# First attention of a two-layer decoder block: scores as three passes of rounded halves instead of one fp32 product

## The reference, cut to what matters

```python
q = rms_norm((x @ wq).reshape(B, L, 16, 128), q_norm_w)
k = rms_norm((x @ wk).reshape(B, L, 4, 128), k_norm_w)
k_ctx = rms_norm((h_ctx_kv @ wk_ctx).reshape(B, T, 4, 128), k_norm_w)
q = q * cos + rotate_half(q) * sin
k = k * cos + rotate_half(k) * sin
k_full = jnp.repeat(jnp.concatenate([k_ctx, k], axis=1), 4, axis=2)
scores = jnp.einsum('blhd,bmhd->bhlm', q, k_full) * scale + mask   # the product that is changed
probs = softmax(scores)
out = einsum('bhlm,bmhd->blhd', probs, v_full) @ wo
```

## Time and profile before

| | |
|---|---|
| three runs | 1883.96, 1883.88, 1882.28 us; median 1883.88 |
| the profiled execution | 1885.15 us, of it a span of 1883.4 us between the first and the last instruction |
| first attention | about the first 1000 us of the span |
| granted TensorE clock | 0.986 of full speed over the span |

### The profile page before, as it was taken

How to read it: one execution, slowest core, us unless ns; L and a number is a source line. 1 busy time by engine, 2 the same in 40 slices (tenths; PEclk the granted TensorE clock), 3 DMA queues, 4 the chain that set the end, 5 groups by cost and what they waited for, 6 DMA issues and landing times. The chain is left out here.

```text
span 1883.4 us, 27617 instructions
## 1 busy us (share of the span) xinstructions
PE 1771.8 (94%) x9732; PEld 1313.5 (70%) x9732; DVE 1093.9 (58%) x2271; ACT 1041.9 (55%) x2318; POOL 961.5 (51%) x864
## 2 busy tenths in 40 slices
PE   7899999999999999999998999989999778879998
PEld 4677777777777777777775888879899656644443
DVE  5554544456445664456655658633433668868886
ACT  3666666655555555555554322136656367857875
POOL 5644565444654445554441100038888356657774
PEclk9999999999999999999999999999999989999999
DMA  7111111211011111011121200157889660000000
GB/s 248 58 48 46 51 36 46 69 33 52 36 40 37 51 53 52 20 34 52 53 68 44 109 23 23 45 183 227 231 224 278 173 162 1 1 6 18 23 23 23
DMA packets 113607, 141.30 MB, mean 75 GB/s; under 512 B 38000, under 2 KB 68720, under 8 KB 113280
## 3 DMA queue, kind: packets, MB, share of 16 engines
q1 hardware_dynamic: 106304, 122.76, 20.7%
q0 software_dynamic: 7168, 16.78, 4.2%
HBM read 104.91 MB, written 29.36 MB: 71 GB/s over the span
## 5 line engine op out<-in xcount | busy, mean ns | idle before, releaser
L767 POOL TENSOR_TENSOR a_xcl<-xT,a_xch 128x512 fp32r<-128x512 f32 x64 | 82.9, 1295 | 282.5 <-ACT a_xch L565 282.5
L876 PE MATMUL a_S<-a_kT,a_qT 128*128 128x288 f32 (+3 forms) x640 | 207.8, 423 | 7.0 <-ACT a_qT L598 5.4
L683 DVE TENSOR_REDUCE a_nmax<-a_S 128x1 f32<-128x192 f32 (+3 forms) x256 | 138.2, 550 | 55.6 <-PE a_S L877 55.2
L934 PE MATMUL a_A<-a_pT,a_vf 128*128 128x512 f32 x320 | 167.0, 604 | 0.9 <-ACT a_pT L586 0.8
L571 ACT ACTIVATE a_pr_odd<-a_S,a_nmax 128x320 f32<-128x320 f32 (+1 forms) x128 | 80.8, 632 | 147.3 <-DVE a_nmax L683 146.0
L876 PEld LDWEIGHTS a_S<-a_kT,a_qT 128*128 128x128 f32 x640 | 115.6, 189 | 52.8 <-issue 23.6
L120 PE MATMUL a_A<-a_wlo,a_xch 128*128 128x512 f32 x256 | 147.3, 575 | 2.7 <-DVE a_qT L679 2.6
L571 ACT ACTIVATE a_pr_even<-a_S,a_nmax 128x192 f32<-128x192 f32 (+1 forms) x128 | 67.2, 527 | 121.2 <-DVE a_nmax L683 120.8
L1592 POOL TENSOR_TENSOR e_wlo<-expert_raw,e_whi 128x1408 fp32r<-128x1408 f32 x31 | 100.4, 3238 | 50.4 <-ACT e_whi L1764 48.3
L2508 PE MATMUL f_HH<-w12T,f_f_xqT 128*128 128x512 bf16 x512 | 120.0, 382 | 4.5 <-DVE a_reco L2322 2.4
L120 PE MATMUL a_A<-a_wlo,a_oth 128*128 128x512 f32 x256 | 112.1, 438 | 7.8 <-DVE a_otl L723 7.8
(11 more groups left out here) (409 smaller groups left out, 5227.6 us busy)
## 6 DMA issues: line engine op xcount, KB each, us to landing
a_pw<-in_L_ffn_w_dram SPq DMA_DIRECT2D x96, 256.0 KB, 2.9
expert_raw<-in_L_ffn_w_gate_dram SPq DMA_DIRECT2D x16, 704.0 KB, 7.6
expert_raw<-in_L_ffn_w_up_dram SPq DMA_DIRECT2D x16, 704.0 KB, 9.7
expert_raw<-in_L_ffn_w_down_dram SPq DMA_DIRECT2D x16, 512.0 KB, 10.3
tern<-a_tern SPq DMA_DIRECT2D x48, 128.0 KB, 1.9
x_res<-in_x_dram SPq DMA_DIRECT2D x4, 1024.0 KB, 9.3
a_raw<-in_L_xattn_wq_dram SPq DMA_DIRECT2D x4, 1024.0 KB, 6.6
a_raw<-in_L_xattn_wo_dram SPq DMA_DIRECT2D x4, 1024.0 KB, 5.4
```

Source lines behind the costliest of these rows:

```text
L683: ve.tensor_reduce(nmax[:, s % 2, i:i + 1], pair(s, i), AX.X, ALU.max, negate=True).then_inc(s_max, 1)
L767: pool.tensor_tensor(xcl[:, t % 2], xT[:, :, tok(t)], xch[:, t % 2].bitcast(F32), ALU.subtract).then_inc(xlo_ready, 1)
L876: pe.matmul(bank[:, lo:hi], qT[:, hq], kT[:, par(t), lo:hi], start=True, stop=hi < nk)
L934: pe.matmul(bank, vf[:, par(t), i], pT[:, i % 2], start=i == 0, stop=False)
```

## The change

The turned q and k are no longer kept as fp32 but as two fp32r halves. They lie in the memory of `xh` and `xl`, which the next stage needs only later: kT_hi and qT_hi in xh, kT_lo and qT_lo in xl. ACT's `k` and `t` write the high halves, of the same shapes as before. DVE gets two new steps, `k` and `t`, that subtract the high half from PSUM (128x128 and 128x512). Once in four slots ACT and DVE split the 64 context columns as well (`l`). Each score product becomes three fp32r passes through `mm3`. `S0` waits for the low halves; so does PE before it uses a bank of a_TR again that a `T` or `K` filled.

```diff
@@ ACT_ORDER, DVE_ORDER
-                 -1: "x v d0 k t r f y",
+                 -1: "x v d0 k t r f l y",
-                 3: "x e0 j0 e1 g0 j1 v e2 r g1 n g2 j2 e3 g3 k t o f"}
+                 3: "x e0 l j0 e1 g0 j1 v e2 r g1 n g2 j2 e3 g3 k t o f"}
-    DVE_SLOT = "M0 M1 N0 L D X v M2 N1 N2 j0 j1 M3 N3 B E A"
+    DVE_SLOT = "M0 M1 N0 L D X l v M2 N1 N2 j0 j1 M3 N3 k t B E A"
-                 0: DVE_SLOT, 1: DVE_SLOT, 2: "M0 M1 N0 L D X v M2 N1 N2 j0 M3 N3 j1 B E A", 3: DVE_SLOT}
+                 0: DVE_SLOT, 1: DVE_SLOT, 2: "M0 M1 N0 L D X v M2 N1 N2 j0 M3 N3 k t j1 B E A", 3: DVE_SLOT}
...
@@ act
+                    if name == "l" and live(s, 1):
+                        t = s + 1
+                        act.wait_ge(ck_loaded, 16 * batch(t))
+                        act.activation(kT_hi[:, par(t), 0:T], kT[:, par(t), 0:T], ACT.Copy).then_inc(ckT_ready, 1)
-                        act.activation(kT[:, par(t), key_cols(t)], TR[:, TR_USE["K", t, 0][0], 0:P], ACT.Copy).then_inc(kT_ready, 1)
+                        act.activation(kT_hi[:, par(t), key_cols(t)], TR[:, TR_USE["K", t, 0][0], 0:P], ACT.Copy).then_inc(kT_ready, 1)
-                        act.activation(qT, TR[:, TR_USE["T", t, 0][0]], ACT.Copy).then_inc(qT_ready, 1)
+                        act.activation(qT_hi, TR[:, TR_USE["T", t, 0][0]], ACT.Copy).then_inc(qT_ready, 1)
...
@@ vector
+                    if name == "l" and live(s, 1) and (s + 1) % BT == 0:
+                        t = s + 1
+                        ve.wait_ge(ckT_ready, batch(t))
+                        ve.tensor_tensor(kT_lo[:, par(t), 0:T], kT[:, par(t), 0:T], kT_hi[:, par(t), 0:T].bitcast(F32),
+                                         ALU.subtract).then_inc(ckT_lo_ready, 1)
+                    if name == "k" and live(s, 1):
+                        t = s + 1
+                        until(ve, kT_ready, tile, t, m)
+                        ve.tensor_tensor(kT_lo[:, par(t), key_cols(t)], TR[:, TR_USE["K", t, 0][0], 0:P], kT_hi[:, par(t), key_cols(t)].bitcast(F32),
+                                         ALU.subtract).then_inc(kT_lo_ready, 1)
+                    if name == "t" and live(s, 1) and i == 0:
+                        t = s + 1
+                        until(ve, qT_ready, tile, t, m)
+                        ve.tensor_tensor(qT_lo, TR[:, TR_USE["T", t, 0][0]], qT_hi.bitcast(F32), ALU.subtract).then_inc(qT_lo_ready, 1)
...
@@ tensor
-                        sem, count = {"P": (pT_ready, turn(before[2])), "T": (qT_ready, tile), "K": (kT_ready, tile),
+                        sem, count = {"P": (pT_ready, turn(before[2])), "T": (qT_lo_ready, tile), "K": (kT_lo_ready, tile),
...
-                            until(pe, qT_ready, tile, t, m)
-                            until(pe, kT_ready, tile, t, m)
+                            until(pe, qT_lo_ready, tile, t, m)
+                            until(pe, kT_lo_ready, tile, t, m)
...
-                            pe.matmul(bank[:, lo:hi], qT[:, hq], kT[:, par(t), lo:hi], start=True, stop=hi < nk)
+                            mm3(pe, bank[:, lo:hi], qT_hi[:, hq], qT_lo[:, hq], kT_hi[:, par(t), lo:hi], kT_lo[:, par(t), lo:hi], True, hi < nk)
                         pe.matmul(bank[:, nk - P:nk], ident_b[:], causal[:], start=False, stop=True).then_inc(s_full, 1)
```

More of the change, by code:

```diff
@@ L150, in attention0_stage @@
                  2: "w x e0 j0 e1 g0 j1 v e2 r g1 n j2 e3 g2 k t o f",
[1 row of a table removed]
-    DVE_SLOT = "M0 M1 N0 L D X v M2 N1 N2 j0 j1 M3 N3 B E A"
-    DVE_ORDER = {"last": "A0 A1 X0 D X1 r0 A2 X2 r1 A3 X3 r2 r3 B", -3: "A0 A1 X0 A2 X1 A3 X2 X3 b u c0 t0 c1 t1", -2: "v A E", -1: "z v X E A", "first": DVE_SLOT,
-                 0: DVE_SLOT, 1: DVE_SLOT, 2: "M0 M1 N0 L D X v M2 N1 N2 j0 M3 N3 j1 B E A", 3: DVE_SLOT}
[1 row of a table added]
+    DVE_SLOT = "M0 M1 N0 L D X l v M2 N1 N2 j0 j1 M3 N3 k t B E A"
+    DVE_ORDER = {"last": "A0 A1 X0 D X1 r0 A2 X2 r1 A3 X3 r2 r3 B", -3: "A0 A1 X0 A2 X1 A3 X2 X3 b u c0 w0 c1 w1", -2: "v A E", -1: "z v X k t E A l", "first": DVE_SLOT,
+                 0: DVE_SLOT, 1: DVE_SLOT, 2: "M0 M1 N0 L D X v M2 N1 N2 j0 M3 N3 k t j1 B E A", 3: DVE_SLOT}
     POOL_ORDER = {"last": "r0 r1 r2 r3", -3: "r0 r1 r2 r3 x w c0", -2: "x c1 r", -1: "q x r", "first": "x q p0 p1 r",
@@ L317, in attention0_stage @@
         kc = q_and_late[:].rearrange("p t (h d) -> p t h d", h=KVH)
-        qT, pT_late = q_and_late[:, 0], q_and_late[:, 1, 0:GH * T]
+        pT_late = q_and_late[:, 1, 0:GH * T]
         causal_in = kT[:, 0, KEYS - P:KEYS]
+        (kT_hi, qT_hi), (kT_lo, qT_lo) = ((flat[:, 0:2 * KEYS].rearrange("p (u n) -> p u n", u=2), flat[:, 2 * KEYS:2 * KEYS + GH * P])
+                                          for flat in (home[:].rearrange("p k n -> p (k n)") for home in (xh, xl)))
         kcT = odd[:, 0:2 * D].rearrange("p (t h n) -> p t h n", t=2, h=KVH)
@@ L342, in attention0_stage @@
         qT_ready, kT_ready = s_.sem("qT_ready"), s_.sem("kT_ready")
+        qT_lo_ready, kT_lo_ready, ckT_ready, ckT_lo_ready = (s_.sem(n) for n in ("qT_lo_ready", "kT_lo_ready", "ckT_ready", "ckT_lo_ready"))
         kv_act, kv_done = s_.sem("kv_act"), s_.sem("kv_done")
@@ L663, in do @@
                         ve.tensor_tensor(wkvl[:], wkv.rearrange("p k a n -> p k (a n)"), wkvh[:].bitcast(F32), ALU.subtract).then_inc(kvl_ready, 1)
-                    if name == "t":
+                    if name == "w":
                         if i == 0:
@@ L866, in do @@
                         if i == 0:
-                            until(pe, qT_ready, tile, t, m)
-                            until(pe, kT_ready, tile, t, m)
+                            until(pe, qT_lo_ready, tile, t, m)
+                            until(pe, kT_lo_ready, tile, t, m)
                             if t % BT == 0:
-                                until(pe, ck_loaded, lambda v: 16 * batch(v), t, m)
+                                until(pe, ckT_lo_ready, batch, t, m)
                                 pe.wait_ge(tab_ready, TABLES)
```

## The result

The changed kernel takes 1885.43 us (median of 20 runs, 1882.27 to 1889.95), the kernel before 1882.74 (20 runs, 1879.29 to 1884.79): a ratio of 1.0015, 95% interval [1.0008, 1.0022]. That is no change by the bound of 0.2%, with the sign on the slower side; the forecast was 1872.0, and the wider of its two ranges ended at 1882. The two profiled executions took 1885.15 before and 1886.9 after.

A forecast was written before the change was run, and what follows sets the result against it. PE was taken as the bound, busy 99.4 of 100 us; 25.3 - 1.6 - 1.2 - 6.4 - 4.2 = 11.9 us gained, so 1872.0 us. Range 1865 to 1879, with rivals 2 to 4 1862 to 1882.

The forecast's parts named there:

- The gross saving: PE's score products, 64 of each length, get shorter by 25.3 us in all; bounds 22 and 29.
- The first rival: 192-column score passes might each cost a whole fp32 product's 0.32 us: +39.4 us, 1911 us; chance 0.12.
- The outcome "slower": Whole kernel slower than before by more than the 0.2% bound; chance 0.14.
- The waits of `W0` behind the 320-column product: Tiles t % 4 = 1: `W0` already waits for `B`, so `S0`'s saving is lost, 16 x 0.10 = 1.6 us.
- `B` behind `t`: Tiles t % 4 = 0: `B` ends later behind `t` and delays `W0`, 15 x 0.08 = 1.2 us lost.
- `j1` behind `t`: Slots 26, 38, 42, 54, 58: quantization step `j1` now follows `t`, delaying `B` and `W0`; 5 x 0.83 = 4.2 us lost.
- tiles with t % 4 = 0 or 3 are covered at `S0`: There `t` ends before PE reaches `S0`, so no new wait; 0.16 us to spare at t % 4 = 0.
- the second rival: PE stands at `S0` in all tiles, `t` 0.35 us late in 31: 11 us gone, about 1883 us; chance 0.15.
- The nine waits at `S0`: Mostly tiles t % 4 = 2, `S0` right after the copy: nine times 0.64 us plus 0.6, 6.4 us lost.
- ScalarE's and VectorE's `l` ... lie far from any wait.: Splitting the 64 context columns, 16 times, 128x64, was taken to delay nothing; no cost counted.
- what PE saves was taken as kept except at the waits named: PE's saving, less the priced losses at `S0`, `W0` and `j1`, passes whole to the end: 11.9 us.
- My third rival: ScalarE and VectorE chains move earlier with PE, so waits absorb less: 21 us gain, 1863 us; chance 0.15.

The follow-up runs named there:

- passes-alone trace: Changed kernel with every score pass on the high halves alone, without VectorE's `k`, `t` and `l`: 1873.04 us, 0.9948 of the kernel before.
- The fillers: Changed kernel plus short bf16 products on PE ahead of the `S0` wait in tiles 0, 18 and 42: 1881.76 us, 0.9995 of the kernel before.
- the last two versions: `j1` between `M3` and `N3`, `g1` ahead of exp 2: in the kernel before 1866.8 us; in the changed kernel, with `l` first too, 1860.73 us.
- both orders: VectorE's `j1` between `M3` and `N3`, ScalarE's `g1` ahead of exp 2 in slots 0 and 3 mod 4; in the kernel before 1866.8 us.
- the version with `g1` ahead: Changed kernel with `l` first in slot -1, `j1` between `M3` and `N3`, and `g1` ahead of exp 2: 1860.73 us, 0.9877 of the kernel before.

## Why the prediction was wrong

**The gross saving was right.** 25.3 us were forecast, 25.7 are there. Pass for pass the estimates stood (0.132, 0.147, 0.203, 0.115 forecast; 0.132, 0.146, 0.203, 0.114 measured). The first rival, a dear 192-column pass, is refuted. The outcome "slower", to which I gave 0.14, came by another way than that rival.

**The steps and the waits that I named were right within a microsecond or so.** `t` takes 0.68 to 0.69 and `k` 0.28. The waits of `W0` behind the 320-column product took 1.6 of 1.6, `B` behind `t` 1.2 to 1.5 of 1.2, and `j1` behind `t` 4.8 of 4.2 in the trace (0.63 lost from tile 27 to tile 28, where a group without `j1` gains 0.33, five times). That tiles with t % 4 = 0 or 3 are covered at `S0` held in all of them but the last, tile 63, which was counted with the nine, and tile 0: the second rival fell too. The nine waits at `S0` took 9.2 us of 6.4, counted from the last mask of the tile ahead to the second of the tile itself against a kernel that keeps its 0.14 us per product; 3.1 of that is the clock behind two of them (the third point below), and the 6.1 left are what was forecast.

**The step that failed first: "ScalarE's and VectorE's `l` ... lie far from any wait."** That holds for the sixteen slots in the loop and not for slot -1, where VectorE has `E` and `A` in front of it and PE nothing to do but tile 0. 4.0 us in the trace; moving it gave 4.8. I had counted the step by its kind and had not looked at its one place at the start.

**The second: what PE saves was taken as kept except at the waits named.** Those named took 5.6 us of the saving: 1.6 of `W0`, some 3.1 at `S0` and 0.9 at `j1`. In the passes-alone trace 13.3 of 25.7 are gone by the last mask, so 7.7 us were missed. One of the places is shown: V1, 0.15 us of it per four tiles, 2 to 3 us in all. I had read only PE's own rows of the view of waits; the kernel before carried this wait in the rows of the weight loads. The other places are read from the trace and were not tried, so their causes stay open: 3.2 us in the first twelve tiles, beside the waits for x and for POOL's rotation, and T's waits for the copy of the turned tail, 3.3 us against 0.4. My third rival ("the waits absorb less") had the sign of this wrong: ScalarE's and VectorE's chains did not move earlier by as much as PE did.

**The third: a wait costs more than itself.** The kernel before has no stretch at less than full clock from 34 to 1010 us; the changed one has three, of about 3.4 us each, behind the waits of 4.25, 2.54 and 1.99 us. The fillers took all three away and with them 3.7 us (4.7 by the masks). No term of mine priced this.

4.0 + 7.7 + 3.7 = 15.4 us. Forecast was a gain of 11.9, found a loss of 3.8 at the last mask: a miss of 15.7. The close fit is partly luck, since the first term is uncertain by 1 us and the third could be 4.7. After the stage about 1.6 us come back, by the rows of `m_LG`.

What remains of the change where the queues suit it is the distance of the last two versions: 1866.8 - 1860.73 = 6.1 us. With both orders in place the waits at `S0` for VectorE are still 10.0 us in nine places, so this is where the next gain would be.

## What to carry to other kernels

An engine that is 99% busy in a stretch is not yet one whose every saved microsecond counts: here work taken off PE was worth 0.3 to 0.5 of itself, and two moves in other engines' queues, with no work saved, were worth 16 us. Before pricing a saving, measure from one fixed instruction to the next in each repeated group (transposes to context product, copy to score) and compare with the same pair elsewhere; a wait of 0.2 us that shows only with the weight loads can be the next one to bind. And read a step's place in the first slot apart from its place in the loop: the step that is free sixteen times can be the only thing that PE waits for at the start.

## What the hardware showed that I had not expected

In the changed kernel the granted clock of TensorE fell to 1.2 GHz after waits of 2.0 to 4.3 us inside a stage in which PE was otherwise nearly always busy (98.35 us of 100 from 200 to 300 us), and came back some 3.4 us later; with filler products in these waits it stayed at 2.4 GHz. The waits of 1.0 to 1.7 us at the other `S0` had no such stretch behind them. But the length of the one wait doesn't decide alone: with the passes alone the clock fell behind a wait of 1.84 us in tile 1 (0.50 from 60 to 62 us), and in the version with `g1` ahead it stayed at 1.00 behind a wait of 2.53 us in tile 18. What else counts is open. By the fillers each such wait cost 1.2 us (a third of the difference of the medians) to 1.6 us (the masks) beyond itself.

An fp32r pass of 192 columns takes 0.114 us and is no cheaper by its columns: 192 are 0.67 of 288, the time is 0.86 of 0.132. Three such passes and one whole fp32 product took the same, 0.32 (the earlier trace rows before, the middle rows of the score products after).
